# Cross attention and a quantized feed-forward layer over 16 sequences: every engine's operations put in another order

## The reference

```
q = layernorm(x) @ Wq;  k = ctx @ Wk;  v = ctx @ Wv
scores = einsum('bhqd,bhkd->bhqk', q, k) * 32 ** -0.5      # k, v repeated for 4 heads each
x = x + (softmax(scores) @ v) @ Wo

y = layernorm(x) in bfloat16
qg, sg = dynamic_quant(y, inv_gate);  qu, su = dynamic_quant(y, inv_up)
gate = (qg @ w_gate.T) * sg * s_wgate;  up = (qu @ w_up.T) * su * s_wup      # 1024 -> 512
inter = clip(silu(gate) * up, -10, 10) in bfloat16
qi, si = dynamic_quant(inter, inv_inter)
x = x + (qi @ w_down.T) * si * s_wdown                                       # 512 -> 1024

dynamic_quant(x, inv): xs = x * inv; scale = max(max|xs| of the row / 127, 1e-8)
                       return clip(round(xs / scale), -127, 127), scale
```

## Time and profile before

| | |
|---|---|
| median of 3 runs | 764.09 us (756.08 to 766.71) |
| the profiled execution | 766.03 us |
| its span in the trace | 764.2 us |
| TensorE busy | 686.0 us (90%), 5840 matmuls |
| VectorE busy | 475.5 us (62%) |
| ScalarE busy | 285.9 us (37%) |
| GpSimd busy | 260.8 us (34%) |
| mean granted TensorE clock | 0.969 of full speed |
| moved by DMA | 93.71 MB |

### The profile page before, as it was taken

The page is one execution under the profiler, slowest core; times in us unless marked ns, Lnnn a source line. Parts: engine busy times, 40 slices in busy tenths (PEclk is TensorE's granted clock), DMA queues, the critical chain, the costliest instruction groups (busy, mean ns, idle before and its releaser), DMA issues.

```text
span 764.2 us, 14196 instructions
## 1 busy us (share of the span) xinstructions
PE 686.0 (90%) x5840; PEld 449.4 (59%) x5840; DVE 475.5 (62%) x772; ACT 285.9 (37%) x449; POOL 260.8 (34%) x207
## 2 busy tenths in 40 slices
PE   3999999989899989999899979999899988997853
PEld 3989888867466646654556646664556543443321
DVE  4562514633566856786747665877647566967863
ACT  4443042373515242435133425253433334343221
POOL 3363130120315134334241534241543235355431
PEclk9999999999999999999989999999999989999967
DMA  9695633769442171235222363233312343211100
GB/s 344 207 364 169 215 98 109 222 216 298 118 167 57 36 223 34 81 94 166 63 80 69 80 177 80 50 101 119 101 47 80 122 118 79 97 57 62 53 27 27
DMA packets 45191, 93.71 MB, mean 123 GB/s; under 512 B 5176, under 2 KB 21560, under 8 KB 45112
## 3 DMA queue, kind: packets, MB, share of 16 engines
q1 hardware_dynamic: 42824, 84.43, 36.0%
q0 software_dynamic: 2304, 8.39, 2.8%
HBM read 70.65 MB, written 22.15 MB: 121 GB/s over the span
## 4 chain that ended last, share of the span: by engine, by line
PE 60%; DMA 21%; SPq 5%; DVE 4%; ACT 4%; POOL 3%; issue 2%; POOLq 0%; ACTq 0%
PE bank L788 14%; PE bank L701 14%; PE bank L814 6%; DMA wv_lo<-r_dram 5%; PE bank L663 4%; PE bank L676 4%; DMA k_stack<-k_dram 4%; DMA max_dram<-max_rows 3%; PE bank_s L720 3%; PE bank L836 3%; PE bank_o L752 3%; PE bank_s L738 3%; PE bank_d L757 3%; DMA r_dram<-r_sb 2%; PE bank L802 1%
## 5 line engine op out<-in xcount | busy, mean ns | idle before, releaser
L701 PE MATMUL bank<-act_t_hi,wq_hi 128*128 128x256 f16 x512 | 140.4, 274 | 0.0
L701 PE MATMUL bank<-act_t_lo,wq_hi 128*128 128x256 f16 x512 | 140.2, 274 | 0.0
L701 PE MATMUL bank<-act_t_hi,wq_lo 128*128 128x256 f16 x512 | 140.1, 274 | 0.0
L2191 DVE TENSOR_REDUCE neg_max<-bank_s 128x4 f16<-128x512 f32 x128 | 84.7, 684 | 54.2 <-PE bank_s L720 53.7
L1622 ACT ACTIVATE probs<-bank_s 128x512 f32<-128x512 f32 x128 | 73.0, 598 | 88.3 <-PE bank_s L738 66.7
L2808 POOL TENSOR_TENSOR wv_hi<-wv_hi,wv_lo 128x512 f32<-128x512 f32 x28 | 37.2, 1334 | 114.5 <-DMA wv_lo<-r_dram 108.2
L1658 ACT COPY q_t<-bank 128x1024 f16<-128x1024 f16 (+1 forms) x48 | 41.8, 871 | 74.3 <-PE bank L802 61.9
L2802 POOL TENSOR_TENSOR xs<-xb,inv_gate 128x1024 f32<-128x1024 bf16 x16 | 35.4, 2211 | 88.0 <-DVE xb L2221 88.0
L738 PE MATMUL bank_s<-q_stack,k_stack 97*128 97x512 f16 x128 | 45.1, 387 | 13.7 <-DMA q_stack<-max_dram 9.1
L701 PEld LDWEIGHTS bank<-act_t_hi,wq_hi 128*128 128x128 f16 x512 | 50.3, 98 | 10.3 <-issue 1.1
L701 PEld LDWEIGHTS bank<-act_t_lo,wq_hi 128*128 128x128 f16 x512 | 50.4, 98 | 9.6 <-issue 0.3
(11 more groups left out here) (145 smaller groups left out, 1372.1 us busy)
## 6 DMA issues: line engine op xcount, KB each, us to landing
q_stack<-q_dram SPq DMA_DIRECT2D x48, 256.0 KB, 4.4
inp<-in_x SPq DMA_DIRECT2D x16, 512.0 KB, 6.0
wv_lo<-r_dram SPq DMA_DIRECT2D x14, 512.0 KB
x<-in_x SPq DMA_DIRECT2D x11, 512.0 KB, 4.2
out<-x POOLq DMA_DIRECT2D x11, 512.0 KB, 3.0
q_dram<-q_st_hi SPq DMA_DIRECT2D x8, 512.0 KB, 4.0
q_dram<-q_st_lo SPq DMA_DIRECT2D x8, 512.0 KB, 5.1
w_gate<-in_ctx_t SPq DMA_DIRECT2D x6, 512.0 KB, 6.4
```

Source lines behind the costliest of these rows:

```text
L701: ins = nc.tensor.matmul(bank[:, :, jj, :], wq_sb[a][:, 2 * item + jj, kc, :], act_t[m][:, kc, :, :], start=(kc == 0 and (a, m) == PARTS[0 ...
L2191: nc.vector.tensor_reduce(neg_max[:, c:c + REP], bank_s[g % 2][:, :].rearrange("p (j n) -> p j n", j=REP), AX_X, ALU.max, negate=True).the ...
```

## The change

Every engine's written list is put in another order. The calls are the same ones on SP (217), ScalarE (448), VectorE (484) and GpSimd (160). On TensorE some `wo_` calls are cut at other chunks, so that 737 calls become 726, with the same matmuls. All helpers, tiles and transfers stay as they are but for one wait in `pv`: with t = 0 it now waits for the reciprocal of the sequence before, and no more for the one of the sequence before that. Of the diff, three pieces of SP's list and this wait are shown; the lists of the other engines change in the same way, nearly all through.

```diff
--- before.py
+++ after.py
...
             spill_q(4)
-            save_r(3, 0)
+            load_res(2, 1)
+            fill_v(3, 1)
+            fill_r(3, 0)
             save_max(3, 1)
             fill_max(3, 1)
-            fill_r(3, 0)
-            load_res(2, 1)
-            fill_v(3, 1)
             fill_q(4, 0)
...
+            fill_v(4, 1)
             save_r(4, 0)
-            spill_q(5)
+            save_max(4, 1)
             fill_r(4, 0)
-            load_x(7, 1)
-            fill_v(4, 1)
             load_x(7, 0)
-            save_max(4, 1)
             fill_max(4, 1)
-            load_res(3, 1)
...
             fill_q(6, 0)
-            fill_k(6, 0)
+            fill_v(6, 0)
             save_r(5, 1)
-            fill_r(5, 1)
-            fill_v(6, 0)
             save_max(6, 0)
             load_res(5, 0)
+            fill_r(5, 1)
             fill_max(6, 0)
             fill_q(6, 1)
             fill_k(6, 1)
+            fill_v(6, 1)
+            load_res(5, 1)
             save_r(6, 0)
-            load_res(5, 1)
             save_max(6, 1)
+            fill_r(6, 0)
             fill_max(6, 1)
-            fill_v(6, 1)
-            fill_r(6, 0)
             spill_q(7)
+            fill_k(7, 0)
             fill_q(7, 0)
-            fill_k(7, 0)
+            save_r(6, 1)
+            fill_r(6, 1)
+            fill_v(7, 0)
             load_res(6, 0)
-            save_r(6, 1)
             save_max(7, 0)
-            fill_v(7, 0)
             fill_max(7, 0)
-            fill_r(6, 1)
+            fill_k(7, 1)
             fill_q(7, 1)
-            fill_k(7, 1)
-            fill_v(7, 1)
             save_r(7, 0)
             fill_r(7, 0)
+            load_res(6, 1)
             save_max(7, 1)
-            load_res(6, 1)
             fill_max(7, 1)
+            fill_v(7, 1)
             load_res(7, 0)
             save_r(7, 1)
             fill_r(7, 1)
...
@@ -744,8 +744,8 @@
                 pe.wait_ge(v_stacked, 16 * (r + 1))
                 if needed(2 * r + t):
                     pe.wait_ge(o_out, 2 * r + t)
-                if t == 0 and needed(r - 1):
-                    pe.wait_ge(recip_done, r - 1)
+                if t == 0 and needed(r):
+                    pe.wait_ge(recip_done, r)
```

More of the change, by code:

```diff
@@ L470, in _ @@
             spill_v(5)
+            spill_k(6)
+            fill_k(0, 1)
+            spill_v(6)
             fill_q(0, 1)
[L472 to L475, removed]
+            spill_k(7)
             load_piece(15)
-            fill_v(0, 1)
[L478 to L483, removed]
+            save_r(0, 0)
+            fill_r(0, 0)
@@ L484, in _ @@
+            load_piece(16)
+            load_piece(17)
+            load_piece(18)
+            fill_v(0, 1)
+            save_max(0, 1)
+            fill_max(0, 1)
+            spill_v(7)
             load_piece(19)
             load_piece(20)
-            spill_v(7)
-            save_max(0, 1)
-            fill_max(0, 1)
             load_piece(21)
-            load_piece(23)
+            load_piece(22)
             sp.wait_ge(k_spilled, 32 * PAIRS)
             sp.wait_ge(v_spilled, 16 * PAIRS)
-            load_piece(22)
+            load_x(3, 0)
@@ L494, in _ @@
+            spill_q(1)
+            load_piece(23)
             load_piece(24)
-            spill_q(1)
-            load_piece(25)
             fill_q(1, 0)
             fill_k(1, 0)
-            load_x(3, 0)
+            load_piece(25)
+            load_piece(27)
             load_piece(26)
-            load_piece(27)
+            load_piece(28)
+            save_r(0, 1)
             fill_v(1, 0)
-            load_piece(28)
+            load_x(3, 1)
+            fill_r(0, 1)
+            save_max(1, 0)
@@ L504, in _ @@
+            load_piece(30)
+            fill_max(1, 0)
             load_piece(29)
[L505 to L508, removed]
             load_piece(31)
-            save_max(1, 0)
-            fill_max(1, 0)
-            fill_r(0, 1)
             load_res(0, 0)
-            load_x(4, 0)
             fill_q(1, 1)
             fill_k(1, 1)
-            spill_q(2)
             load_res(0, 1)
+            save_max(1, 1)
             fill_v(1, 1)
@@ L520, in _ @@
             load_x(4, 1)
+            load_x(4, 0)
+            fill_max(1, 1)
             save_r(1, 0)
+            spill_q(2)
+            load_res(1, 0)
             fill_r(1, 0)
-            save_max(1, 1)
-            fill_max(1, 1)
             fill_k(2, 0)
@@ L527, in _ @@
             save_r(1, 1)
+            fill_v(2, 0)
+            save_max(2, 0)
             fill_r(1, 1)
-            save_max(2, 0)
-            fill_v(2, 0)
             fill_max(2, 0)
@@ L533, in _ @@
             fill_q(2, 1)
+            fill_k(2, 1)
+            save_r(2, 0)
+            load_res(1, 1)
+            fill_r(2, 0)
             load_x(5, 1)
-            fill_k(2, 1)
-            load_res(1, 1)
+            spill_q(3)
             fill_v(2, 1)
-            spill_q(3)
-            save_r(2, 0)
-            fill_r(2, 0)
             save_max(2, 1)
@@ L545, in _ @@
             save_r(2, 1)
+            load_res(2, 0)
             fill_r(2, 1)
-            load_res(2, 0)
+            fill_v(3, 0)
             save_max(3, 0)
             fill_max(3, 0)
-            fill_v(3, 0)
-            load_x(6, 0)
             fill_q(3, 1)
@@ L1534, in _ @@
+            wo_(6, 1, 1, 4, 7)
+            st(7, 1, 2)
+            wo_(6, 1, 1, 7, 8)
             ti(5, 1)
-            st(7, 1, 1)
-            st(7, 1, 2)
+            st(7, 1, 3)
             dn(5, 1, 0)
@@ L2927, in _ @@
             norm(4, 0, 0)
+            norm(4, 0, 1)
+            o_lo(4, 0, 0)
             xs_(3, 0, 1)
+            fin(2, 1)
             rstd1_(7, 0)
-            o_lo(4, 0, 0)
-            norm(4, 0, 1)
-            rstd1_(7, 1)
-            fin(2, 1)
             o_lo(4, 0, 1)
@@ L2936, in _ @@
             xs_(3, 1, 0)
+            norm(4, 1, 0)
             xs_(3, 1, 1)
-            norm(4, 1, 0)
             norm(4, 1, 1)
+            rstd1_(7, 1)
             o_lo(4, 1, 0)
+            fin(3, 0)
             o_lo(4, 1, 1)
-            fin(3, 0)
             rstd2_(4, 0)
```

1594 lines of the change are left out of this document (794 added, 800 removed).

## The result

The changed kernel takes 790.2 us in the median of four runs (786.5 to 793.9), the kernel before 763.6 beside it; the ratio is 1.036 (1.027 to 1.044). The forecast was 774 with a range of 742 to 790, so the time lies just outside. The profiled execution's span grew from 764.2 to 792.1 us, by 27.9.

What follows compares the result with a forecast made beforehand. Bound by TensorE's fixed work plus its idle time. Terms -6.5 - 4.8 - 2.7 + 28.1 + 1.7 - 7 + 1 = +9.8 on the profiled 766.0 give 775.8, a median of 774 us; range 742 to 790.

Steps and rivals of the forecast that it cites:

- 1, k_stack: k and q fills, `st`(r,7) to `s`(r+1,0): more TensorE cover removes nearly all 7.2 us of waiting; -6.5 us.
- 2, v_cur: The v_cur load held behind `fill_r` on SP's queue now stands ahead of it, so its wait goes; -4.8 us.
- 3, inter: `code_i(5, 0)` behind `o_hi_(6, 1, 0)` on ScalarE: `fill_r` issued earlier ends TensorE's wait for inter; -2.7 us.
- Step 4: Row-max round trip, `mt`(r) to `st`(r,0): `fill_r` between or ahead of the pair holds the small q_stack load; +28.1 us.
- Step 5: TensorE's clock: four waits of 5 to 7 us each lose 3.4, 13.6 against 11.9 before; +1.7 us.
- step 4's second group: r = 2, 7, 14 and 15, `fill_r` issued ahead of `save_max`: `fill_max` lands late, 2.5 us each, 10.0 us.
- Step 6: Small TensorE waits, 12.4 us between 60 and 680: other engines catch up while TensorE waits; -7 us.
- Step 7: The end: `fin(6, 0)` moved, `ln2_stats(7, 0)` ahead of an awaited quantization, otherwise the same operations; +1 us (-1 to +2).
- That the small load isn't held: Rival: q_stack load not held behind `fill_r`, 24.3 us shrinks to 0, clock returns 8; 742 us (736 to 750), chance 0.20.
- That the small waits go and step 4's second group costs nothing: Rival: `fill_r` is through before `save_max` and all small waits go; 759 us (750 to 765), chance 0.18.
- That the reciprocals come late: Rival: late `recip` on VectorE puts `fill_r` fully on six row-max pairs, 15 us more; 789 us (780 to 796), chance 0.18.

Runs made afterwards that it cites:

- the fastest kernel: Changed kernel with `fill_r` in four DMAs, the start put back and the whole end in the old order; 735.7 us, ratio 0.961.
- five calls put back: Changed kernel with `fill_r` in four DMAs, the start put back and only five calls of the end in the old order; 739.4 us, ratio 0.965.

## Why the prediction fell short, step by step

The direction of the forecast (slower than before) and its main mechanism held, and the size did not: +9.8 us were forecast for the span's side, +27.9 came. By its own steps, in us:

| step | forecast | measured |
|---|---|---|
| 1, k_stack | -6.5 | -7.2, no row left |
| 2, v_cur | -4.8 | -4.8 |
| 3, inter | -2.7 | -2.3, 0.4 left before the end |
| 4, row maxima | +28.1 | +25.5 |
| 5, clock | +1.7 | +6.2 |
| 6, small waits | -7 | +3.3 |
| 7, the ends | +1 | +7.6 |
| sum | +9.8 | +28.3 (span: +27.9) |

**Step 4** was right in kind and nearly in size. The four pairs with `fill_r` between them waited 4.77, 6.50, 6.65 and 3.09, in all 21.0 us, for 24.3; the four with `fill_r` ahead 3.94, 1.70, 3.75 and 2.21, 11.6 for 10.0; two others 2.0 for 2.9. The single load at r = 12 took 10.39 us for my 10.0. The rule of the Trainium skill on k ("DMA: Bandwidth & Descriptors", section "Why a DMA increments its semaphore by 16 and not by 1") bears this out: by it one DMA with four groups outermost sits on four engines, two DMAs of two groups on the same two, and a DMA of 32 rows on 16. The trace agrees: the busy shares of the 16 engines are 0.25, 0.13 and 0.99, and the order of the measured times, 9.4, 14.2 and 4.6 us, is the one that this gives, where no count of DMAs or bytes gives it. The small load is one packet of 8 KB in the trace, with one more for the semaphore (2 packets, 0.01 MB, from 649.97 to 651.6 in the changed kernel), so it is on one engine; on which, no view shows, but it was held at all four r. What I took from the same page of the Trainium skill, section "Queues, rings and completion order", that the ring's order holds the small load, is at most a third of it here: with a queue of their own, eleven of the fourteen `save_max` on the chain still took 4.3 to 6.9 us, each of these eleven issued 0.5 to 6.8 us behind a `fill_r`, and what is saved at r = 12 is 3 us of the 9.4 that the load was held, with nothing saved for the pair at r = 4, 9 and 13. So the forecast of this step was right by the engines, and only in a small part by the queue's order that it named.

**Step 5** counted four waits. But the clock also fell at the waits of step 4's second group, and elsewhere: nine stretches with a part at half of full speed, for five. I had priced these waits at 10.0 us in one step and left them out of the next. The price itself was also read wrongly in the other direction: 23.8 against 11.9 us by the granted clock, 11.9 more, but TensorE's busy time, where a matmul at 1.2 GHz shows as a longer one, grew by 6.2, since part of each stretch lies in a wait, where TensorE has nothing to do (the window 419 to 421 above has a clock of 0.50 and no matmul). The term was mis-sized, +1.7 for +6.2 by busy time. With the four pairs mended it came back (682.7 us busy), and in the fastest kernel there is less busy time than before the change (674.0).

**Step 6** failed outright, and it is the largest miss, 10.3 us. I argued that the other engines catch up while TensorE waits, so that small waits go; the window of the earlier trace rows was one good stretch and no evidence on the others. What idles in the middle without q_stack, k_stack, v_cur and inter was 17.1 us before (40.9 less 23.8) and is 20.4 in the changed kernel (55.4 less 34.6 and 0.4), 2.5 of the growth being xb's longer wait ahead of the last `wo_`. Without the long waits it is 19.0 (`fill_r` in four) and 15.5 (the fastest kernel). So these waits belong to the order and not to the state of the other engines: long waits neither bring nor take them.

**Step 7** was not looked at closely enough. The start lost 3.5 us by the order of the first calls of GpSimd and ScalarE (`rstd1_` by the rows above; what ScalarE's share is was not tried alone); I compared SP's first five loads, which are the same, and stopped there. In the end, rows of the changed kernel from the last `wo_` on (VectorE, GpSimd, VectorE, TensorE):

```profile
753.16 1.22 DVE L2215 TENSOR_REDUCE amax<-xs 128x1 f32<-128x1024 f32 x1 [1.59 <-POOL xs L2791]
...
756.85 2.68 POOL L2791 TENSOR_TENSOR xs<-xb,inv_up 128x1024 f32<-128x1024 bf16 x1 [3.72 <-ACT code_g L1668]
757.58 2.24 DVE L2255 TENSOR_SCALAR inter<-u_buf 128x512 bf16<-128x512 f32 x1
...
762.89 0.61 PE L824 MATMUL bank<-ident,inter 128*128 128x128 f16 x4 [7.91 <-ACT inter L1672]
```

`quant(7, 1, 0)` (its L2215) stands ahead of `swiglu(7, 0)` and `quant_i(7, 0)`, and these are the chain to inter that TensorE waits for, 7.91 us where it was 5.64. I had said that the chain of the last two sequences has the same operations; it has, in another order. The end took 61.4 us for 57.3.

**The rivals.** That the small load isn't held fell. That the small waits go and step 4's second group costs nothing fell with steps 4 and 6. That the reciprocals come late gives almost the measured time, 789, but by another way: of its six pairs, those of r = 6 and 8 did not wait at all, and the other four waited 11.6 us, not the 20 that it asks for. It was not the cause, and its closeness to 790.2 is chance. The wait of `pv` for the later reciprocal cost nothing that could be measured, as said.

What stays open: why five calls put back did not give the end its old time, while the whole old order did. The difference between these two kernels is `ln2_stats(7, 1)`, `ln2_apply(7, 1)`, `resid_(7, 1, 0)` and two `rstd2_`; which of them it is wasn't tried. The traces show where the time sits: from the last `wo_` on, with `fill_r` in four, TensorE idles 27.5 us with the five calls and 24.8 with the whole old order, and is busy 33.5 and 32.9. Its wait for g_buf, 1.7 us, is there only in the first, and its waits for xb are 2.0 for 0.6. So most of the 3.3 us are waits for VectorE's and GpSimd's work on the last two sequences, and at most 0.6 can be the clock's.

## What to carry to other kernels

Look at a DMA's outermost dimension before its place in the order: a broadcast load written with four groups outermost took 9 us and held the small loads issued in that time, while 128 partitions in four DMAs took half of that, and this one edit was worth more (2.8 per cent in the kernel before) than a new order of 2,000 calls. A small load that the busiest engine waits for must not be issued within the time that such a transfer runs, and another queue hardly frees it. When a forecast sums waits, each wait goes through the clock's term as well, and small waits are taken as they are, unless a run shows that they go.

## What the runs showed of the hardware

VectorE and GpSimd slow each other more than their busy shares tell. In the rows of the end above, the clipping of inter (L2255) takes 2.24 us beside GpSimd's `xs_`, itself 2.68 for 2.13; alone it takes 0.43, as in the ends of the kernel before and of the fastest one. At the start the normalization takes 2.61 us when it begins behind `ctx` (which runs from 12.55 to 14.66) and 0.81 when it begins ahead of it. It is so in the middle of every kernel too: of the 16 clippings in the kernel before, the four that begin while a GpSimd operation runs take 1.26 to 2.35 us and end 0.3 us after it, and the others take 0.43. So VectorE's operation looks held until GpSimd's is through. An operation that the old order kept clear of GpSimd can grow by 1.8 us in a new one, and its duration in a trace of the old order is then not the one to sum.
